# One half of a block's up product: two pieces of one batch each, or two pieces of two batches each between later units

## The chip, the cores and the metric

The kernel runs on 1 core of one Trainium2 chip. The metric is the device time of one execution in microseconds (us), the median of several runs. The core has a matmul engine (TensorE, PE in the profile), a vector engine (VectorE, DVE), a scalar engine (ScalarE, ACT), GpSimd (POOL) and a DMA-issuing engine (SyncE, SP). Each engine works through its own list of instructions in order, and the lists wait for one another by semaphores.

## The reference, cut to what matters

Four batches of 128 rows with 512 features (512 tokens in all) pass through one layer: cross attention to 2048 context rows of each batch, causal self attention with 16 heads over a compressed query, key and value, and a feed-forward part with a shared expert of 1024 inner features and 16 routed experts of 256, of which each token takes four. Each of the three parts adds to the rows.

```python
def relu2(x):
    return jnp.square(jax.nn.relu(x))
...
x = x + _L0_xattn_ref(_layernorm(x, axis=-1), ctx_768, ...)
x = x + _L0_attn_ref(_layernorm(x, axis=-1), ...)
x = x + _L0_ffn_ref(_layernorm(x, axis=-1), ...)
...
shared = relu2(x2 @ shared_up.T) @ shared_down.T
out = routed + shared
```

The change concerns `x2 @ shared_up.T`, for the first 256 of the 1024 inner features and the first 256 of the 512 tokens.

## The kernel before, in words

The shared expert is cut into four blocks of 256 inner features. A block's up product has 256 inner features (two tiles of 128, `m` = 0 and 1) and sums over 512 features (four chunks of 128, `c`). Every float product is made in three matmuls (`split_mm`, line 1604): both operands are kept as a high part and a remainder, and high times low, high times high and low times high are summed in PSUM. So one tile `m` takes 4 x 3 = 12 matmuls whatever the number of tokens, and each has a weight load of its own.

For blocks 0 and 1 the up product is cut by tokens too: the half of batches 0 and 1 (256 tokens), which fits into one PSUM bank for both tiles `m`, is computed while the self attention of the later batches is still running; the other half comes after it. `up_half(e, h, m)` (line 1717) computes tile `m` of half `h` of block `e` in 12 matmuls with 256 columns of tokens. `up_rows(e, m, b)` (line 1728) computes tile `m` for batch `b` alone, in 12 matmuls with 128 columns. Before, block 0's first half is made by `up_rows`, batch 0 first and batch 1 later; block 1's first half by `first_up` (line 1737), which calls `up_half`.

Self attention is cut into 16 units, four for each batch, each of four heads. For a unit, in order:

- TensorE computes its scores, two units at a time (`pair_scores`, line 1750), into one of the banks that `hs_bank` (line 426) names in turn. `pair_scores(14)` waits until `unit_exp(12)` has read the bank before it.
- VectorE masks them and finds the row maxima (`mask_and_max`, line 1116).
- ScalarE takes the exponentials (`unit_exp`, line 847: four pairs of an ACTIVATE and a read of the accumulator, L856).
- VectorE inverts the sums (`inverse_sums`, L1125), and GpSimd multiplies the weights by them (`unit_weights`, L631).
- TensorE transposes the weights into the one bank `B_W` (`unit_T`, line 1765, L1772), after ScalarE has copied out the unit before, and ScalarE copies them out (`unit_copy`, line 841, L845).
- After each batch's four units TensorE multiplies by the values (`unit_sums`, line 1823, L1831), ScalarE and VectorE take the result's two parts (`attended_hi`, L835, and `attended_lo`, L1331), and TensorE projects it (`project`, line 1835).

The order of all this is written out by hand, one list for each engine. TensorE's list around the change is in the program below, from `sums_T(3)` on. ScalarE's list in the same stretch is `unit_exp(12)`, the copy of transposed rows for batch 1 (`rows_hi`, L749), `unit_copy(10)`, `unit_copy(11)`, `unit_exp(13)`, `router_exp(1)`, `attended_hi(2)`, `unit_exp(14)`, `unit_copy(12)`, `unit_exp(15)`, and the copies of units 13 to 15. Then comes `relu_half(0, 0)` (line 772, L777), the first reader of the up product, which waits for semaphore `up_mm`.

GpSimd makes the remainder of block 0's up weights (`half_low`, line 639, L643), and `rows_lo` (line 1095, L1097) the remainder of the normalised rows; both are operands of the product.

Of the kernel before, what the change touches and what calls it, by code (L numbers as in the profile page):

```python
# [25 lines left out]
P = 128  # L26
# [10 lines left out]
def layer_program(nc, x, ctx_in, ctxT_in, wqT, wkT, wv, wd, wu, woT, experts, bq, bk, bv, gate, bias_e,  # L37
                  gammas_betas, out):
    NB, S, D = x.shape
    NKEY, TD = ctx_in.shape[1:]  # L40
    DC = D // P
# [12 lines left out]
    IC = 2  # L54
# [24 lines left out]
    with ExitStack() as es:  # L79
        def sb(name, shape, dt=F32):  # L80
            return es.enter_context(nc.sbuf_tensor(name, shape, dt))
# [7 lines left out]
        def sem(name):  # L89
            return es.enter_context(nc.semaphore(name))  # L90
# [27 lines left out]
        xT_h = sb("xT_h", [P, DC, T], F32R)  # L118
        xT_l = sb("xT_l", [P, DC, T], F32R)
# [91 lines left out]
        def aT(b, i):  # L211

            return (aT_first if b < NB // 2 else aT_last)[:, i, :]
# [12 lines left out]
        def hw_of(u):  # L226

            return hw[:, u % 2, :] if u < 2 * ROWS else hw_more[:, u % 4, :]

        def u_part(e, i):  # L230

            return u_w[e][:, i, :]
# [48 lines left out]
        def small(name, shape, dt=F32):  # L281
# [36 lines left out]
        bank = [es.enter_context(nc.psum_tensor(f"bank{i}", [P, 512], F32)) for i in range(8)]  # L318
# [16 lines left out]
        var_ok, rstd_ok, xn_ok, xT_mm, xhi_ok, xlo_ok = (sem(n) for n in ("var_ok", "rstd_ok", "xn_ok", "xT_mm", "xhi_ok", "xlo_ok"))  # L335
# [7 lines left out]
        qkv_mm, qkv_ok, hs_mm, hnb_ok, exp_ok, hrd_ok, hw_ok, hwT_mm, hwT_ok, a_mm, ahi_ok, alo_ok, wo_mm, x2_ok = (sem(n) for n in (  # L343
            "qkv_mm", "qkv_ok", "hs_mm", "hnb_ok", "exp_ok", "hrd_ok", "hw_ok", "hwT_mm", "hwT_ok", "a_mm", "ahi_ok", "alo_ok", "wo_mm", "x2_ok"))
        lg_mm, rexp_ok, sel_ok, cnt_mm, cnt_ok, ent_ok, ent_mm, idx_ok = (sem(n) for n in (
            "lg_mm", "rexp_ok", "sel_ok", "cnt_mm", "cnt_ok", "ent_ok", "ent_mm", "idx_ok"))
        up_mm, relu_ok, sq_ok, g_ok, acc_mm, base_ok, y_out = (sem(n) for n in (
            "up_mm", "relu_ok", "sq_ok", "g_ok", "acc_mm", "base_ok", "y_out"))
# [10 lines left out]
        ulo_first, dlo_first = sem("ulo_first"), sem("dlo_first")  # L359
# [6 lines left out]
        def tok(b):  # L366
            return slice(b * S, (b + 1) * S)
# [19 lines left out]
        def rows_bank(b):  # L387

            return 1 if b < NB - 1 else B_S

        def wo_bank(b):

            return 1 if b == NB - 2 else B_S
# [4 lines left out]
        HT_TOK = T // 2  # L398
# [4 lines left out]
        def half_bank(e, h):  # L403

            return B_UP[e][0] if h else B_UP[0][e]

        def half(h):
            return slice(h * HT_TOK, (h + 1) * HT_TOK)
# [26 lines left out]
        def unit_at(step, lag):  # L435
# [5 lines left out]
        order = sorted([(POST + 1 + NCH * b, "middle", b) for b in range(NB)] +  # L441
                       [(WO_STEP + 1 + NCH * b, "last", b) for b in range(NB)])
        norm_no = {(kind, b): NB + i for i, (_, kind, b) in enumerate(order)}

        PAIR, COPIED = 2, NQ - 1
# [1155 lines left out]
        def _(pe):  # L1601
            mm = nc.tensor.matmul

            def split_mm(dst, a, b, start, stop):

                mm(dst, a[0], b[1], start=start, stop=False)  # L1606
                mm(dst, a[0], b[0], start=False, stop=False)  # L1607
                return mm(dst, a[1], b[0], start=False, stop=stop)  # L1608

            def rows_T(n, dst):  # L1610
                pe.wait_ge(xn_ok, n + 1)
                for c in range(DC):
                    last = nc.tensor.transpose(dst[:, c * P:(c + 1) * P], xn[:, n % 2, c * P:(c + 1) * P], ident[:])
                last.then_inc(xT_mm, 1)
# [34 lines left out]
            for h in range(DC):  # L1649
                for i in range(2):  # L1650
                    last = mm(bank[B_ROW][0:2, 0:TDB], bq2[:, h, :], wk2[:, i, h, :], start=h == 0 and i == 0, stop=h == DC - 1 and i == 1)
# [11 lines left out]
            for part in range(2):  # L1663
                pe.wait_ge(xlo_ok, 2 * part + 2)
                o = slice(part * HB, (part + 1) * HB)
                for c in range(DC):
                    for t in range(TC):
                        if part == 0:
                            pe.wait_ge(mlo_ok, min(c + 1 + (c == 0 and t == 2), DC))
                        last = split_mm(bank[B_QK[part][t]][:, 0:HB], (M2[:, 0, c, t * P:(t + 1) * P], M2[:, 1, c, t * P:(t + 1) * P]),  # L1670
                                        (xT_h[:, c, o], xT_l[:, c, o]), c == 0, c == DC - 1)
# [5 lines left out]
            for c in range(DC):  # L1677
                mm(bank[B_ROW][0:2, :], M2[:, :, c, TD], xT_h[:, c, :], start=c == 0, stop=False)
                last = mm(bank[B_ROW][0:2, :], M2[:, :, c, TD], xT_l[:, c, :], start=False, stop=c == DC - 1)
# [37 lines left out]
            def up_half(e, h, m):  # L1717

                pe.wait_ge(ulo_first, 2 * e + 2)
                for c in range(DC):  # L1720
                    o = c * IC * P + m * P
                    last = split_mm(bank[half_bank(e, h)][:, m * HT_TOK:(m + 1) * HT_TOK],
                                    (u_part(e, 0)[:, o:o + P], u_part(e, 1)[:, o:o + P]),
                                    (xT_h[:, c, half(h)], xT_l[:, c, half(h)]), c == 0, c == DC - 1)
                if m == IC - 1:
                    last.then_inc(up_mm, 1)

            def up_rows(e, m, b):

                for c in range(DC):  # L1730
                    o = c * IC * P + m * P
                    last = split_mm(bank[half_bank(e, 0)][:, m * HT_TOK + b * S:m * HT_TOK + (b + 1) * S],
                                    (u_part(e, 0)[:, o:o + P], u_part(e, 1)[:, o:o + P]),
                                    (xT_h[:, c, tok(b)], xT_l[:, c, tok(b)]), c == 0, c == DC - 1)
                return last

            def first_up(e, m):
                pe.wait_ge(xlo_ok, norm_no["last", 1] + 1)
                pe.wait_ge(exp_ok, UNITS - 2)
                up_half(e, 0, m)  # L1740
# [9 lines left out]
            def pair_scores(u):  # L1750

                b, r = divmod(u, ROWS)
                pe.wait_ge(qkv_ok, 3 * b + 2)
                if u > 2 * ROWS:
                    pe.wait_ge(exp_ok, u - 1)
                elif u >= 2:
                    pe.wait_ge(exp_ok, u)
                for j in range(HT):
                    for i in range(2):
                        rows = slice((r + i) * DH, (r + i + 1) * DH)  # L1760
                        o = slice(j * P, (j + 1) * P)
                        last = mm(bank[hs_bank(u + i)][:, o], qk_s[rows, 0, o], qk_s[rows, 1, o], start=True, stop=True)  # L1762
                last.then_inc(hs_mm, 2)

            def unit_T(u, step=TAIL):
                pe.wait_ge(hw_ok, u + 1)
                if step - LAG < G:
                    pe.wait_ge(wT_ok, step - LAG + 1)
                else:
                    pe.wait_ge(hwT_ok, u)  # L1770
                for j in range(HT):
                    last = nc.tensor.transpose(bank[B_W][:, j * P:(j + 1) * P], hw_of(u)[:, j * P:(j + 1) * P], ident[:])  # L1772
                last.then_inc(hwT_mm, 1)
# [61 lines left out]
            def project(b):  # L1835
                pe.wait_ge(w_lo, LO_O)
                pe.wait_ge(alo_ok, b + 1)
                if b < 2:
                    pe.wait_ge(qkv_ok, 3 * (b + 2))
                elif b < NB - 1:  # L1840
                    pe.wait_ge(rexp_ok, b)
                else:
                    pe.wait_ge(qkv_ok, 3 * NB)
                for j in range(HT):
                    last = split_mm(bank[wo_bank(b)][:], (aT(b, 0)[:, j * P:(j + 1) * P], aT(b, 1)[:, j * P:(j + 1) * P]),
                                    (wo_w[:, 0, j * D:(j + 1) * D], wo_w[:, 1, j * D:(j + 1) * D]), j == 0, j == HT - 1)
                last.then_inc(wo_mm, 1)
# [45 lines left out]
            for step in range(1, TAIL):  # L1893
# [22 lines left out]
                if 0 <= g < G:  # L1916
                    b, c = divmod(g, NCH)
# [4 lines left out]
                    for k in range(KT):  # L1922
                        last = mm(bank[B_O][:, 0:TD], wT[:, g % 2, k * P:(k + 1) * P], ring[:, g % RING, k, :],  # L1923
                                  start=(c == 0 and k == 0), stop=(c == NCH - 1 and k == KT - 1))
# [29 lines left out]
            unit_T(10)  # L1954
            pe.wait_ge(rexp_ok, 1)
            rows_T(norm_no["last", 1], bank[rows_bank(1)])
            pe.wait_ge(ulo_first, 2)
            pe.wait_ge(xlo_ok, norm_no["last", 0] + 1)
            pe.wait_ge(qkv_ok, 3 * NB - 1)
            for m in range(IC):  # L1960
                up_rows(0, m, 0)
            pair_scores(14)
            unit_T(11)
            router(1)
            unit_sums(2)
            unit_T(12)
            pe.wait_ge(xlo_ok, norm_no["last", 1] + 1)
            for m in range(IC):
                last = up_rows(0, m, 1)
            last.then_inc(up_mm, 1)  # L1970
            unit_T(13)
            project(2)
            unit_T(14)
            first_up(1, 0)
# [164 lines left out]
            for b in range(NB):  # L2139
                for i in range(NL):  # L2140
                    pe.wait_ge(ylo_ok, i + 1)
                    mm(bank[B_END[b]][:], of_token[:, i, tok(b)], ys_h[:, (NG - NL + i) % NYS, :], start=False, stop=False)
                    last = mm(bank[B_END[b]][:], of_token[:, i, tok(b)], ys_l[i][:], start=False, stop=i == NL - 1)
# [53 lines left out]
```

## Time and profile before

| | us |
|---|---|
| median of 3 runs | 352.87 |
| lowest and highest run | 352.58, 354.71 |
| span of the profiled execution, first to last instruction | 350.9 |
| TensorE busy in that span | 332.0 |
| VectorE busy | 239.4 |
| ScalarE busy | 190.5 |

The profile shows one execution. It gives the span and no separate time for that execution; the median of the runs lies 2.0 us over the span. A busy time counts an instruction from its start to its end, and matmuls overlap in the pipeline, so the distance between the starts of neighbouring matmuls tells more of their cost than the duration of one. The chain of work is followed back from the last instruction: at each step to what released it, or to the instruction before it on its engine.

### The profile page before, as it was taken

Reading aid. Unit: us, or ns where it says so; the run is one execution under the profiler, and the core shown is the slowest. Engines: PE = TensorE matmul, PEld = TensorE weight load, DVE = VectorE, ACT = ScalarE, POOL = GpSimd, SP = SyncE. Lnnn points to the kernel's source line nnn. Section 1 sums busy time; section 2 is a strip of 40 time slices with the busy share of each in tenths; the row PEclk is TensorE's granted clock in tenths of the full one; section 3 lists DMA queues with packets and bytes.
Section 4 is the critical chain, followed back from the end, with each engine's and each line's share of the span. In section 5 each row is a group of like instructions: output and inputs, shape, how many; then the busy total and the mean of one; then the engine's idle time right before and its main releaser. Section 6 shows DMA issues by size and latency. Waiting matters only on the chain.

```text
span 350.9 us, 7040 instructions
## 1 busy us (share of the span) xinstructions
PE 332.0 (95%) x2554; PEld 235.1 (67%) x2554; DVE 239.4 (68%) x475; ACT 190.5 (54%) x428; POOL 98.4 (28%) x114
## 2 busy tenths in 40 slices
PE   6999989999999998999799899999999999999995
PEld 4988756677777755867689789788544444444453
DVE  2885789655489637748975469980556777778486
ACT  2356765525576476466777454302246777777510
POOL 3600400000001311226584140004446865522000
PEclk9899999999999999999999999999999999999999
DMA  7985499986422227018032471799834463321483
GB/s 228 401 336 177 180 370 404 412 282 197 156 99 90 92 91 290 40 45 346 2 121 92 150 270 32 297 375 398 326 104 164 166 205 133 119 96 62 157 323 120
DMA packets 17185, 69.70 MB, mean 199 GB/s; under 512 B 2816, under 2 KB 3328, under 8 KB 14592
## 3 DMA queue, kind: packets, MB, share of 16 engines
q1 hardware_dynamic: 12768, 56.93, 43.2%
q0 software_dynamic: 3520, 11.54, 9.3%
q10 hardware_dynamic: 864, 0.79, 0.7%
q8 instruction: 21, 0.34, 0.4%
q14 instruction: 12, 0.10, 0.1%
HBM read 61.91 MB, written 7.34 MB: 197 GB/s over the span
## 4 chain that ended last, share of the span: by engine, by line
PE 71%; DVE 15%; ACT 7%; issue 4%; DMA 2%; DVEq 0%; POOL 0%; ACTq 0%
PE bank L2068 10%; PE bank L2100 10%; PE bank L1923 8%; PE bank L1606 8%; PE bank L1608 8%; PE bank L1607 8%; PE bank L2037 3%; PE bank L1815 2%; DVE res L1583 2%; DMA raw<-in_wkT 2%; PE bank L1867 2%; PE bank L1772 2%; DVE cT L1296 1%; PE bank L1762 1%; PE bank L2079 1%
## 5 line engine op out<-in xcount | busy, mean ns | idle before, releaser
L1923 PE MATMUL bank<-ring,wT 128*128 128x384 f32 x128 | 44.0, 487 | 0.7 <-ACT wT L898 0.7
L2068 PE MATMUL bank<-WX,xsT 128*32 128x256 f32 (+1 forms) x256 | 36.4, 380 | 0.0
L2100 PE MATMUL bank<-WX,hsT 128*32 128x512 f32 (+1 forms) x128 | 36.2, 595 | 0.0
L692 POOL DMA_INDIRECT xs<-x_rows,from_row x20 | 22.1, 1108 | 48.9 <-DVE to_row L1250 25.2
L1296 DVE TENSOR_TENSOR cT<-ring_T,cT 128x512 fp32r<-128x512 f32 x45 | 30.0, 710 | 6.5 <-ACT cT L756 6.5
L1923 PEld LDWEIGHTS bank<-ring,wT 128*128 128x128 f32 x128 | 23.6, 190 | 14.2 <-ACT wT L898 0.9
L1530 DVE COPY copy<-WX 128x1024 f32 x32 | 21.1, 703 | 13.1 <-PE bank L2100 5.9
L2068 PEld LDWEIGHTS bank<-WX,xsT 128*32 128x32 f32 x256 | 17.1, 110 | 18.8 <-issue 8.4
L756 ACT CAST cT<-ring_T 128x512 fp32r<-128x512 f32 x48 | 27.0, 619 | 4.6 <-PE bank L1608 4.5
L2068 PE MATMUL bank<-copy,xsT 128*32 128x256 f32 x384 | 29.3, 380 | 0.0
L2100 PE MATMUL bank<-copy,hsT 128*32 128x512 f32 x192 | 29.1, 595 | 0.0
L602 POOL TENSOR_TENSOR rstd<-var,mhalf 128x1 f32<-128x1 f32 x12 | 7.5, 625 | 73.3 <-DVE var L1082 73.2
L1537 DVE COPY copy<-WX 128x1024 f32 x32 | 21.4, 711 | 5.9 <-PE bank L2068 3.9
L1506 DVE COPY xsT<-bank 128x512 f32<-128x512 f32 x20 | 13.1, 685 | 14.4 <-PE bank L2037 14.4
L699 POOL DMA_INDIRECT y_rows<-ys,to_row x16 | 18.3, 1142 | 12.8 <-ACT ys L1004 10.1
L2100 PEld LDWEIGHTS bank<-WX,hsT 128*32 128x32 f32 x128 | 8.2, 109 | 20.2 <-issue 19.9
L1028 ACT COPY copy<-WX 128x1024 f32 x16 | 16.8, 1048 | 8.3 <-PE bank L2100 7.1
L1606 PE MATMUL bank<-cT,qk_h 128*128 128x512 f32 x48 | 20.0, 417 | 0.2 <-POOL cT L620 0.2
L1608 PE MATMUL bank<-cT,qk_l 128*128 128x512 f32 x48 | 18.8, 393 | 0.0
L1607 PE MATMUL bank<-cT,qk_h 128*128 128x512 f32 x48 | 18.8, 391 | 0.0
L1606 PE MATMUL bank<-xT_l,u_w 128*128 128x256 f32 (+2 forms) x56 | 17.9, 320 | 0.0
L1607 PE MATMUL bank<-xT_h,u_w 128*128 128x256 f32 (+2 forms) x56 | 17.4, 312 | 0.0
(296 smaller groups left out, 883.4 us busy)
## 6 DMA issues: line engine op xcount, KB each, us to landing
WX<-in_experts SPq DMA_DIRECT2D x16, 1024.0 KB, 6.9
ring_T<-in_ctxT SPq DMA_DIRECT2D x16, 768.0 KB, 7.3
ring<-in_ctx SPq DMA_DIRECT2D x16, 768.0 KB, 5.1
WX<-y_rows SPq DMA_DIRECT2D x4, 1024.0 KB, 8.1
raw<-in_experts SPq DMA_DIRECT2D x3, 1024.0 KB, 5.0
raw<-in_wqT SPq DMA_DIRECT2D x4, 256.0 KB, 5.7
res<-in_x SPq DMA_DIRECT2D x4, 256.0 KB, 8.1
raw<-in_woT SPq DMA_DIRECT2D x1, 1024.0 KB, 5.8
```

The lines of the kernel that those rows point to most:

```text
L692: nc.gpsimd.indirect_dma_start(out=xs[:, s % NXS, :], out_offset=None, in_=x_rows, in_offset=bass.IndirectOffsetOnAxis(ap=from_row[:, s:s ...
L699: nc.gpsimd.indirect_dma_start(out=y_rows, out_offset=bass.IndirectOffsetOnAxis(ap=to_row[:, s:s + 1], axis=0), in_=ys[:, s % NYS, :], in_ ...
L756: copy(cT[:, g % 2, 0, t, :], ring_T[:, g % RING_T, t, :]).then_inc(cThi_ok, 1)
L1296: V_.tensor_tensor(cT[:, g % 2, 1, t, :], ring_T[:, g % RING_T, t, :], f32(cT[:, g % 2, 0, t, :]), ALU.subtract).then_inc(cTlo_ok, 1)
L1530: V_.tensor_copy(copies[n % NC][:], WX[:, bass.ds(middle[g][q - 1] * (2 * HALF), HALF)]).then_inc(up_copied, 1)
L1537: V_.tensor_copy(copies[n % NC][:], WX[:, bass.ds(values[q - 1] * (2 * HALF) + HALF, HALF)]).then_inc(down_copied, 1)
L1606: mm(dst, a[0], b[1], start=start, stop=False)
L1607: mm(dst, a[0], b[0], start=False, stop=False)
L1608: return mm(dst, a[1], b[0], start=False, stop=stop)
L1923: last = mm(bank[B_O][:, 0:TD], wT[:, g % 2, k * P:(k + 1) * P], ring[:, g % RING, k, :], start=(c == 0 and k == 0), stop=(c == NCH - 1 an ...
L2068: last = mm(bank[B_H[g % 2]][q * SLOT:(q + 1) * SLOT, 0:IC * P], xsT[:, g % 2, c * P + q * SLOT:c * P + (q + 1) * SLOT], w, start=c == 0, ...
L2100: last = mm(bank[B_Y[g % 2]][q * SLOT:(q + 1) * SLOT, :], hsT[:, g % 2, m * P + q * SLOT:m * P + (q + 1) * SLOT], w, start=m == 0, stop=m ...
```

## The change

The function for one batch goes. Block 0's first half is computed by `up_half` in two pieces, one for each tile `m`, both after unit 12: one between units 12 and 13, the other between units 13 and 14. The piece that stood between the transposes of batch 1's rows and `pair_scores(14)` has nothing in its place.

```diff
-            def up_rows(e, m, b):
-
-                for c in range(DC):
-                    o = c * IC * P + m * P
-                    last = split_mm(bank[half_bank(e, 0)][:, m * HT_TOK + b * S:m * HT_TOK + (b + 1) * S],
-                                    (u_part(e, 0)[:, o:o + P], u_part(e, 1)[:, o:o + P]),
-                                    (xT_h[:, c, tok(b)], xT_l[:, c, tok(b)]), c == 0, c == DC - 1)
-                return last
-
...
             unit_T(10)
             pe.wait_ge(rexp_ok, 1)
             rows_T(norm_no["last", 1], bank[rows_bank(1)])
-            pe.wait_ge(ulo_first, 2)
-            pe.wait_ge(xlo_ok, norm_no["last", 0] + 1)
-            pe.wait_ge(qkv_ok, 3 * NB - 1)
-            for m in range(IC):
-                up_rows(0, m, 0)
             pair_scores(14)
             unit_T(11)
             router(1)
             unit_sums(2)
             unit_T(12)
             pe.wait_ge(xlo_ok, norm_no["last", 1] + 1)
-            for m in range(IC):
-                last = up_rows(0, m, 1)
-            last.then_inc(up_mm, 1)
+            pe.wait_ge(qkv_ok, 3 * NB - 1)
+            up_half(0, 0, 0)
             unit_T(13)
+            up_half(0, 0, 1)
             project(2)
             unit_T(14)
             first_up(1, 0)
```

## Rows read from the trace of the kernel before

**Rows 1.** The page: span, and busy time of each engine.

```profile
span 350.9 us, 7040 instructions
...
PE 332.0 (95%) x2554; PEld 235.1 (67%) x2554; DVE 239.4 (68%) x475; ACT 190.5 (54%) x428; POOL 98.4 (28%) x114
```

**Rows 2.** The page: the chain that ended last, by engine.

```profile
PE 71%; DVE 15%; ACT 7%; issue 4%; DMA 2%; DVEq 0%; POOL 0%; ACTq 0%
```

**Rows 3.** The chain in order of time around the change: start us, us, what.

```profile
176.49 0.04 issue
176.53 1.16 PE bank L1762 x16
...
180.11 0.06 PE bank L1606
...
182.74 1.09 PE bank L1762 x16
183.83 0.58 PE bank L1772 x4
...
185.66 1.01 PE bank L1831 x32
186.66 0.59 PE bank L1772 x4
187.25 0.06 PE bank L1606
...
189.88 0.46 PE bank L1772 x4
190.34 0.23 PE bank L1606
...
193.52 0.12 PE bank L1606
...
194.93 0.44 PE bank L1772 x4
```

**Rows 4.** PE by line and shape, 179 to 206 us: mean ns of one.

```profile
L1606 PE MATMUL bank<-xT_l,u_w 128*128 128x128 f32 x16 | 4.5, 279 | 0.0
...
L1606 PE MATMUL bank<-xT_l,u_w 128*128 128x256 f32 x8 | 2.4, 302 | 0.0
```

**Rows 5.** ACT in order of time, 181 to 196 us.

```profile
181.83 0.21 ACT L856 ACTIVATION_READ_ACCUMULATOR hw_more<-bank,hnb 128x1 f32 x1
...
182.39 0.62 ACT L845 COPY hwT_last<-bank 128x512 f32<-128x512 f32 x1
...
186.73 0.59 ACT L835 CAST aT_last<-bank 128x512 fp32r<-128x512 f32 x1 [0.21 <-PE bank L1831]
...
188.60 0.61 ACT L845 COPY hwT_last<-bank 128x512 f32<-128x512 f32 x1
...
195.89 0.61 ACT L777 ACTIVATE act<-bank 128x512 f32<-128x512 f32 x1
```

**Rows 6.** DVE in order of time: remainder of batch 1's rows, mask of unit 14.

```profile
182.68 0.66 DVE L1097 TENSOR_TENSOR xT_l<-bank,xT_h 128x512 fp32r<-128x512 f32 x1
183.88 0.69 DVE L1105 SCALAR_TENSOR_TENSOR masked<-bank,upper 128x512 uint8<-128x512 f32 x1 [0.54 <-PE bank L1762]
```

**Rows 7.** POOL in order of time: the weights of unit 13.

```profile
186.74 1.04 POOL L631 TENSOR_TENSOR hw_more<-hw_more,hrd 128x512 f32<-128x512 f32 x1 [1.57 <-DVE hrd L1125]
```

**Rows 8.** PE in order of time, first 10 us: its longest wait between matmuls.

```profile
7.82 0.95 PE L1630 MATMUL bank<-wk,UW 128*128 128x386 f32 x4 [1.74 <-ACT UW L787]
```

**Rows 9.** Stretches: engines' busy times, then granted clock (1.00 is full), DMA share, GB/s.

```profile
9.00:10.00 1.00, 0.84 (x3) 0.84 (x4) 0.70 (x2) 0.63 (x2) 0.58 (x1) 0.64 1.09 390
10.00:12.00 2.00, 2.00 (x8) 2.00 (x7) 1.56 (x5) 1.78 (x4) 1.52 (x2) 0.50 1.09 418
12.00:13.00 1.00, 1.00 (x6) 1.00 (x5) 0.97 (x5) 0.00 (x0) 0.85 (x1) 0.65 0.99 410
198.00:200.00 2.00, 1.11 (x7) 0.81 (x6) 0.69 (x1) 1.98 (x4) 0.00 (x0) 1.00 1.01 379
```

## The prediction

> **What bounds the kernel now.** I read the page's busy times first: TensorE is busy for 332.0 of 350.9 us, the next engine for 239.4 [rows 1]. The reader is to see that only TensorE can be the bound of the whole, and then to distrust the 95%: a matmul's busy time overlaps its neighbours', so the engine can be busy by the page and still wait inside that time, and a cheaper instruction is not worth its busy time. Second comes the chain that ended last: 71% of it is TensorE, 15% VectorE, 7% ScalarE [rows 2]. Third, the chain in order of time around the edit: from 180.11 us to 194.93 us each piece is TensorE's, with no hole, and both pieces that the change takes out lie on it [rows 3]. So before, TensorE's own list sets the time there, and what is saved on it counts until another engine's result is awaited. The question is therefore which result comes last once the list is shorter, and the three lists of ScalarE, VectorE and GpSimd answer it [rows 5 to 7].
>
> **What goes and what comes, on TensorE alone.** Removed are two pieces of 24 matmuls with 128 columns. The first runs from 180.11 to 182.74, the second from 187.25 to 189.88, 2.63 us each, which is 0.110 us for a matmul [rows 3]. Added are two pieces of 12 matmuls with 256 columns. The same function already runs for block 1: 12 matmuls from 193.52 to 194.93, 1.41 us, 0.117 us for each [rows 3]. So twice the columns cost 7 ns more, and TensorE is spared 2 x 2.63 - 2 x 1.41 = 2.44 us. The durations of one, 279 and 302 ns, would have given 48 x 0.279 - 24 x 0.302 = 6.1 us; they overlap and are not the price [rows 4].
>
> A rule of the Trainium skill speaks against the saving. Its page TensorE: Matmul & The Clock Gate, section Back-to-back issue gap, gives the isolated distance of two matmuls as the columns over 2.4 GHz and 2.5 ns more, thus about 56 ns at 128 columns and 109 ns at 256; by it 48 x 0.056 = 2.7 us would go and 24 x 0.109 = 2.6 us would come, an estimate by that page, and the change would only move work. The trace does not agree at 128 columns: it shows 110 ns there, twice that figure.
>
> **First wait, between 180.11 and `pair_scores(14)`.** The piece for batch 0 stood in a place where TensorE would otherwise have waited. `pair_scores(14)` overwrites the bank that `unit_exp(12)` reads, and the last accumulator read of that unit ends at 181.83 + 0.21 = 182.04 [rows 5]. From the end of a ScalarE result to TensorE's next work the chain shows 0.04 us, and the 16 score matmuls then take 1.16 us [rows 3]. So after the change they run from 182.08 to 183.24, where before they ended at 183.83: of the 2.63 us removed here, 0.59 are gained and 1.97 become a wait from 180.11 to 182.08. What ends there is not itself moved: `unit_exp(12)` hangs on `mask_and_max(12)`, ahead of everything that waits for `pair_scores(14)` in VectorE's list.
>
> **The stretch after it moves 0.59 us forward.** `unit_T(11)` 0.58 (to 183.82), the router of batch 1 184.41 to 185.66, thus 1.25 (to 185.07), `unit_sums(2)` 1.00 (to 186.07), `unit_T(12)` 0.59 (to 186.66) [rows 3]. None of these meets another wait: `unit_T(11)` needs the copy that ends at 182.39 + 0.62 = 183.01 [rows 5], the router the remainder that ends at 182.68 + 0.66 = 183.34 [rows 6]. VectorE's mask of unit 14 started 0.05 us after the scores, at 183.88 [rows 6], so it follows them forward to 183.29. Then the first new piece takes 1.41 (to 188.07). Its waits are long met: the high rows, weights and bank that it needs were ready for the piece before.
>
> **Second wait, between the first new piece and `unit_T(13)`.** There is one bank for the transposes, and `unit_T(13)` needs `unit_copy(12)` to have emptied it. That copy is not late because of `unit_T(12)`. It stands in ScalarE's list behind `attended_hi(2)` and `unit_exp(14)`, and before it ran from 188.60 to 189.21 [rows 5]. `attended_hi(2)` starts at 186.73, 0.06 us after `unit_sums(2)` ended [rows 3, 5], so this run of ScalarE moves forward by the same 0.59: the copy runs from 188.01 to 188.62, and TensorE goes on at 188.66. Before, the 2.63 us piece covered this copy with 0.67 us to spare (it ended at 189.88). The new one is 1.22 us shorter, and 0.59 us of waiting appears (188.07 to 188.66). GpSimd's weights of unit 13 are no rival here: they ended at 186.74 + 1.04 = 187.78 before and follow forward [rows 7].
>
> Behind the waiting `unit_T(13)` in TensorE's list stand the second new piece, `project(2)` and `unit_T(14)`. They need nothing later than that copy. So: 188.66 + 0.46 (`unit_T(13)`) + 1.41 (second piece) = 190.53. Before, `project(2)` began at 190.34 [rows 3]. The sum: 2.44 us of work saved, 1.97 + 0.59 us of new waits, and 0.07 us more for scores that start from a standstill (1.16 against 1.09) [rows 3]; together 0.19 us later.
>
> **What hangs on the moved pieces besides.** The up product is now complete at 190.53, not 189.88. Its reader on ScalarE starts at 195.89, behind the copies of units 13 to 15 [rows 5], so 5.4 us of cover remain. The step issues no DMA and passes no queue of SP or GpSimd. From 190.53 on the order is as before, and the chain runs through TensorE, so I carry 0.19 us to the end undiminished: 350.9 + 0.2 = 351.1 for the span. The profiled span lies 2.0 us under the median of the runs, which I take as unchanged: 353.1 us.
>
> **Bounds of what no row shows.** The two waits don't exist before. The first is certain to some hundredths, since its releaser does not move. The second hangs on five ScalarE instructions keeping their distances. If the copy came early enough the wait would vanish and `project(2)` start 0.59 us sooner, 0.4 us earlier than before; if ScalarE fell behind by as much, 0.8 us later. With these ends the median would be 352.5 to 353.7. I take the middle, since all distances on ScalarE come from rows.
>
> **Rivals.**
>
> *The saving comes through whole.* If neither wait lasted, 2.44 us would be gained: 350.4 us. For it: the stretch is all TensorE on the chain. Against it: `unit_exp(12)` ends at 182.04 whatever TensorE does [rows 5].
>
> *The clock falls in the first wait (the slower side).* The longest wait between matmuls before is 1.74 us, up to 7.82 us [rows 8]; from then on the granted clock went from full to 0.50 and came back. The stretches 9 to 13 us show 0.64, 0.50, 0.50 and 0.65, which at two levels (1.00, that is 2.4 GHz, and 0.50, 1.2 GHz) is 0.72 + 2.00 + 0.70 = 3.4 us at the lower one, with half of it lost, 1.7 us [rows 9]. The new wait, 1.97 us, is longer than that one. If it has the same effect, the work behind it takes 1.7 us longer, ScalarE's list follows, and the time is 353.1 + 1.7 = 354.8 us. Against it: the early wait came in the first 8 us of the kernel, while here the chain shows the engine at work without a hole up to the wait, and after it [rows 3]. At 198 to 200 us it worked for only 1.11 of 2 us, and the clock stayed at 1.00 [rows 9]. It decides from the point at which the clock falls at all; a shorter first wait would not show it.
>
> The Trainium skill's page on TensorE, section HAM oscillation — how this bites in real kernels, describes kernels in which waits between bursts of matmuls send the clock down each time. The trace agrees with it at 9 us and shows no such fall later.
>
> *The wide pieces cost by their columns*, so that 256 cost twice 110 ns: each new piece would take 2.64 us, the second wait would vanish, and `project(2)` would start at 186.66 + 2.64 + 0.46 + 2.64 = 192.40, 2.1 us late: 355.0 us. The rows of block 1's pieces at 117 ns are nearly proof against it [rows 3].
>
> **How the numbers follow.** I give 0.80 to the forecast, whose own range is 352.4 to 353.8; 0.08 to the whole saving; 0.10 to the fallen clock; 0.02 to the wide pieces' price. The runs before spread from 352.58 to 354.71, skewed upward. The range that should hold 8 in 10 goes from 352.0, half way to the whole saving, to 354.8, the fallen clock. A measurement of this kernel tells about 1%, or 3.5 us, from no change. No case reaches it on the faster side: all of the work saved is 2.44 us, so 0.02. On the slower side a fallen clock that lasts twice as long would come near, so 0.03. That leaves 0.95 for no change.
>
> **What would show each step right or wrong.** Right: 24 matmuls of 256 columns about 0.117 us apart for block 0; a TensorE wait of about 2 us before the scores of units 14 and 15, released by ScalarE's exponentials (L856); a second of about 0.6 us before `unit_T(13)`, released by the copy at L845; `project(2)` within 0.5 us of 190.5; the granted clock at 1.00 throughout. Wrong: the first wait under 1.5 us, the second missing, a granted clock below 1.00 between 182 and 188 us, or a shift that is there at 190 us and gone at the end.

## The result and the profile after

The changed kernel takes 355.63 us (median of 22 runs, 353.15 to 357.21); the kernel before, run beside it, takes 353.09 us (22 runs, 351.75 to 354.71). The ratio is 1.006, with a 95% interval of 1.0043 to 1.0076: slower by 0.6%. The profiled execution took 356.8 us, with a span of 355.0 us. In every ratio here the runs more than 1.5% over the fastest of their kernel are left out; for three of the experiments (e3_gap_only, e4_early, f1_split) that takes out the long runs which they are about, so there the median of all runs is what counts.

The page of the changed kernel, span and busy times, to be held against [rows 1]:

```profile
span 355.0 us, 6992 instructions
...
PE 335.5 (95%) x2530; PEld 237.6 (67%) x2530; DVE 239.8 (68%) x475; ACT 190.6 (54%) x428; POOL 97.8 (28%) x114
```

TensorE has 24 matmuls less and is busy for 3.5 us more. Something has made its instructions longer. The chain in order of time shows where (L1753 are the scores, L1763 the transposes of a unit, L1822 the sums of a batch):

```profile
180.78 1.25 ACT hw_more L856 x7
182.03 0.14 issue
182.17 2.08 PE bank L1753 x16
184.24 1.04 PE bank L1763 x4
185.29 0.01 PE bank L1606
...
187.65 1.87 PE bank L1822 x32
189.52 1.05 PE bank L1763 x4
190.56 0.21 PE bank L1606
...
192.66 0.44 PE bank L1763 x4
193.10 0.12 PE bank L1606
...
194.51 0.23 PE bank L1606
```

Against [rows 3] the reader is to see the same list of work at nearly twice the price: the scores take 2.08 us and not 1.16, unit 11 takes 1.04 and not 0.58, the sums 1.87 and not 1.01. From 192.66 us on all has its old price: unit 13 takes 0.44, and the second wide piece behind it goes from 193.10 to 194.51, 1.41 us. `project(2)` begins at 194.51, where before it began at 190.34, 4.17 us later; the two spans differ by 4.1 us.

The waits of TensorE, the longest first:

```profile
PE bank L1753 <- ACT hw_more L856: 2.4, 1, 2.4
PE bank L1618 <- DVE wT L1265: 1.5, 1, 1.5
```

The new wait is now the longest of all. The stretches around it in the changed kernel (engines' busy times, then the granted clock, DMA share, GB/s):

```profile
164.00:169.00 5.00, 4.58 (x52) 3.58 (x49) 4.55 (x8) 3.15 (x11) 2.64 (x3) 0.66 0.06 25
169.00:180.00 11.00, 9.66 (x69) 7.47 (x67) 8.43 (x22) 7.82 (x25) 5.83 (x7) 1.00 0.02 8
180.00:182.00 2.00, 0.00 (x0) 0.00 (x0) 1.93 (x5) 1.48 (x9) 1.95 (x3) 0.93 0.45 131
182.00:184.00 2.00, 1.83 (x16) 1.81 (x16) 1.32 (x3) 0.99 (x3) 2.00 (x3) 0.50 0.87 324
184.00:186.00 2.00, 2.00 (x12) 1.83 (x10) 1.65 (x3) 0.67 (x2) 1.14 (x1) 0.50 0.41 172
186.00:188.00 2.00, 2.00 (x16) 1.95 (x20) 1.14 (x3) 1.50 (x9) 0.39 (x1) 0.50 0.71 236
188.00:190.00 2.00, 2.00 (x35) 1.54 (x24) 1.55 (x3) 0.42 (x1) 0.65 (x1) 0.50 0.07 27
190.00:192.00 2.00, 2.00 (x11) 2.00 (x10) 0.87 (x2) 2.00 (x11) 0.13 (x1) 0.51 0.00 0
```

And in the profile of the kernel before:

```profile
180.00:190.00 10.00, 10.00 (x120) 9.59 (x120) 8.29 (x16) 7.81 (x35) 6.67 (x7) 1.00 0.55 180
```

After the change TensorE does nothing from 180 to 182 us, the clock goes to the lower level (0.50, 1.2 GHz) inside that stretch, at 181.7 us, and stays there until 192 us: 0.28 + 8.00 + 1.96 = 10.2 us. TensorE is busy in all of the eight microseconds from 184 on, and they count as no hole in the chain. There is another low stretch, 3.4 us between 164 and 169 us, ahead of the change; what it costs is read below.

### The profile page after: what moved, and what is told of

Its sections match the earlier page's. It is cut to its first block, busy times and chain, and to the rows that moved or that the text cites. A ratio compares the mean times of both kernels' runs of the same rounds, so it can differ in the third digit from the quotient of the medians.

```text
span 355.0 us, 6992 instructions
## 1 busy us (share of the span) xinstructions
PE 335.5 (95%) x2530; PEld 237.6 (67%) x2530; DVE 239.8 (68%) x475; ACT 190.6 (54%) x428; POOL 97.8 (28%) x114
## 4 chain that ended last, share of the span: by engine, by line
PE 70%; DVE 16%; ACT 7%; issue 3%; DMA 2%; POOL 1%; DVEq 0%; ACTq 0%
PE bank L2054 10%; PE bank L2086 10%; PE bank L1914 8%; PE bank L1606 8%; PE bank L1608 7%; PE bank L1607 7%; PE bank L2023 3%; DVE res L1583 2%; DMA raw<-in_wkT 2%; PE bank L1806 2%; PE bank L1858 2%; PE bank L1763 1%; DVE cT L1296 1%; PE bank L1822 1%; PE bank L1753 1%
## 5 line engine op out<-in xcount | busy, mean ns | idle before, releaser
L1028 ACT COPY copy<-WX 128x1024 f32 x16 | 16.8, 1047 | 8.3 <-PE bank L2086 7.1
L1033 ACT COPY copy<-WX 128x1024 f32 x16 | 16.7, 1042 | 0.0
L1606 PE MATMUL bank<-xT_l,u_w 128*128 128x256 f32 (+1 forms) x48 | 16.4, 341 | 0.0
```

## The experiments

Two theories stand against each other. **A:** the wait ahead of the scores lets TensorE's clock fall, and the light steps behind it (16 score matmuls of 32 rows, four transposes, 12 router matmuls of 16 columns, the sums) leave it low. **B:** the new order costs the time by its two waits on ScalarE, and the clock is a bystander. Each kernel is compared with the kernel before on the same chip. The median of the kernel before alone goes from 353.09 to 354.24 us between the rows, so times are compared inside a row, and rows by their ratios.

| run | edit | us, median of all (range) | kernel before | ratio and interval |
|---|---|---|---|---|
| changed kernel | | 355.63 (353.15 to 357.21) | 353.09 | 1.006 (1.0043 to 1.0076) |
| e1_fill17 | wait filled, 17 matmuls | 354.34 (353.71 to 355.03) | 353.39 | 1.0029 (1.0014 to 1.0045) |
| e1_fill8 | wait filled, 8 matmuls | 355.22 (353.24 to 357.72) | 354.24 | 1.0035 (1.0007 to 1.0063) |
| e2_mixed | one tile in the early place | 354.07 (353.30 to 358.57) | 353.39 | 1.0033 (1.0004 to 1.0062) |
| e3_gap_only | kernel before, early piece left out | 358.83 (353.25 to 360.75) | 353.39 | 1.003 (0.999 to 1.0069) |
| e4_early | wide pieces one place earlier | 353.83 (352.40 to 360.31) | 353.39 | 1.001 (0.9981 to 1.0039) |
| f1_split | wide pieces between light steps | 354.22 (351.37 to 357.61) | 353.81 | 0.9972 (0.9947 to 0.9997) |
| f2_split_fill | f1_split and filled | 353.49 (351.81 to 354.62) | 353.81 | 0.9997 (0.9974 to 1.002) |

**The wait filled** (against the changed kernel).

```diff
             rows_T(norm_no["last", 1], bank[rows_bank(1)])
+            pe.wait_ge(ulo_first, 2)
+            pe.wait_ge(xlo_ok, norm_no["last", 0] + 1)
+            pe.wait_ge(qkv_ok, 3 * NB - 1)
+            for _ in range(17):
+                mm(bank[half_bank(0, 0)][:, 0:P], u_part(0, 0)[:, 0:P], xT_h[:, 0, tok(0)], start=True, stop=True)
             pair_scores(14)
```

> The changed kernel with 17 matmuls of 128 columns whose result is overwritten, put where the piece for batch 0 stood (1.9 us of work in a wait of 2.0 us; nothing of the product is left out). Theory A, the clock: with TensorE at work there, the granted clock stays at 1.00 from 180 to 195 us; project(2) starts near 190.5 us as forecast, and the time is 0.998 to 1.002 of the kernel before. Theory B, the order: the two waits on ScalarE cost the time by themselves and the clock is a bystander; the ratio stays at 1.006.

The order and its dependences on ScalarE are those of the changed kernel, TensorE has 17 matmuls more to do, and the time is less, by the ratios (1.0029 against 1.006) some 1.1 us. B's 1.006 lies outside the interval: that speaks against B. But A's number was missed too, 1.0029 where at most 1.002 was expected, and so was its full clock. The stretches of the profiled run say why:

```profile
180.00:182.00 2.00, 1.73 (x16) 1.59 (x15) 1.97 (x4) 1.39 (x9) 1.96 (x3) 1.00 0.39 135
182.00:184.00 2.00, 1.74 (x23) 1.65 (x23) 1.92 (x5) 1.08 (x4) 2.00 (x3) 1.00 0.87 311
184.00:186.00 2.00, 2.00 (x33) 1.98 (x35) 1.60 (x3) 1.95 (x10) 1.24 (x2) 0.86 0.47 197
186.00:188.00 2.00, 2.00 (x26) 1.62 (x18) 1.86 (x4) 1.15 (x6) 1.04 (x1) 0.50 0.75 240
188.00:190.00 2.00, 2.00 (x15) 2.00 (x15) 1.12 (x3) 2.00 (x12) 0.76 (x1) 0.79 0.06 23
```

The clock now holds through the wait's place, of which 0.53 us is left, and falls later, at 185.4 us, for 3.4 us: through the sums and the transposes of unit 12 and into the first wide piece. TensorE had been at work without a hole since the scores began at 182.26 us. So a fall without the long wait is seen here; the kernel before shows one without any wait further down.

Half the filler, 8 matmuls in place of 17:

> The changed kernel with 8 matmuls of 128 columns in the first wait in place of 17 (0.9 of 2.0 us filled, a wait of about 1.1 us stays; nothing of the product is left out). Theory A, the clock goes with the length of the wait: the median lies between the filled kernel and the changed one, ratio 1.003 to 1.006, and runs above 356 us are rare. Theory B: 1.006 as in the changed kernel.

By its ratio, 1.0035, this kernel can't be told from the filled or from the changed one. In its profile a wait of 1.23 us is left, and the clock is low for 6.8 us (0.98, 0.50, 0.50, 0.50, 0.82 over the five stretches of 2 us from 182 to 192 us), between the 3.4 and the 10.2 us of the other two. One of its 11 runs was above 356 us; 7 of the changed kernel's 22 were.

**The wait alone** (against the kernel before). This kernel does not compute block 0's up product for batch 0.

```diff
-            for m in range(IC):
-                up_rows(0, m, 0)
             pair_scores(14)
```

> The kernel before with batch 0's piece left out and nothing in its place (the up product of block 0 for batch 0 is not computed): the first wait alone, without any piece of 256 columns and without the second wait. Theory A, the clock: the wait of 2 us brings the clock down as in the changed kernel, and the ratio is 1.003 to 1.006 although TensorE does 2.6 us less work. Theory B, the order: 24 matmuls are saved, the scores start 0.6 us earlier, there is no second wait, and the ratio is 0.997 to 0.999.

Block 0 has no piece of 256 columns here and there is no second wait, TensorE has 24 matmuls less than before, and the median of all its runs is 5.4 us higher (358.83 against 353.39), the largest difference of all the runs. Eight of the twelve took over 358 us; none of the 35 runs of the kernel before beside them took over 354.82. TensorE's wait and the clock of the profiled run, 360.75 us:

```profile
182.62 0.80 PE L1762 MATMUL bank<-qk_s 32*128 32x128 f32 x4 [2.38 <-ACT hw_more L856]
```

```profile
182.00:192.00 10.00, 9.38 (x75) 8.69 (x75) 6.76 (x12) 5.58 (x26) 4.63 (x5) 0.52 0.45 157
192.00:200.00 8.00, 8.00 (x32) 7.33 (x32) 0.35 (x2) 2.50 (x11) 2.08 (x2) 0.53 0.01 2
```

The low stretch lasts some 17 us here (9.6 of the ten microseconds, then 7.5 of eight), two thirds longer than in the changed kernel, and it outlasts the piece for batch 1 behind unit 12, whose 24 matmuls of 128 columns run from 191.01 to 196.03 us, nearly twice their price; it ends at 199.5 us among the 512-column matmuls of `project(2)`. B wanted 0.997 to 0.999. The ratio of 1.003 does not quite exclude that, as its interval begins at 0.999; the medians and the profile go against B. The size was not foreseen by A either.

**One tile in the early place** (against the kernel before). Tile 0 for batch 0 stays where it was, tile 1 becomes one wide piece.

```diff
-            for m in range(IC):
-                up_rows(0, m, 0)
+            up_rows(0, 0, 0)
             pair_scores(14)
...
-            for m in range(IC):
-                last = up_rows(0, m, 1)
-            last.then_inc(up_mm, 1)
+            up_rows(0, 0, 1)
+            up_half(0, 0, 1)
             unit_T(13)
```

> Tile 0 as in the kernel before (batch 0 in the early place, batch 1 after unit 12), tile 1 as one piece of 256 columns after unit 12, both ahead of unit 13. Theory A, the clock: 12 matmuls fill 1.3 of the 2.0 us, a wait of about 0.7 us stays, the clock holds, the scores of units 14 and 15 start 0.6 us earlier than before, TensorE's list is 1.2 us shorter, and project(2) starts at about 189.9 instead of 190.3: ratio 0.998 to 0.999, and lower than the changed kernel by 0.7%. Theory B, the order: the scores start as in the changed kernel, so the ratio is 1.004 to 1.006.

The scores did start early, at 181.92 us after a wait of 1.0 us, yet the ratio is 1.0033: a miss for A as I had put it, and no verdict against B, whose 1.004 to 1.006 lies inside the interval. In its profile the clock held through the wait and then was low for 3.4 us from 184.8 us, as in the filled kernel: the long fall is missing there, the short one is not. Three of the twelve runs, of 355.69 to 358.57 us, were longer, and none of them has a profile.

**Wide pieces among the light steps** (against the changed kernel). The first variant moves each piece up by one place, the second also puts the router behind unit 12, and the third adds the 17 fillers to the second.

```diff
             unit_T(11)
-            router(1)
-            unit_sums(2)
-            unit_T(12)
             pe.wait_ge(xlo_ok, norm_no["last", 1] + 1)
             pe.wait_ge(qkv_ok, 3 * NB - 1)
             up_half(0, 0, 0)
-            unit_T(13)
+            unit_sums(2)
+            unit_T(12)
+            router(1)
             up_half(0, 0, 1)
+            unit_T(13)
             project(2)
```

The diff is that of f1_split, in which ScalarE's `router_exp(1)` goes behind `unit_copy(12)`; in e4_early the router stays ahead of the sums and ScalarE's list as it was.

> The changed kernel with the two pieces of 256 columns moved up by one place each: the first right behind unit 11, ahead of the router and the sums of batch 2, the second behind unit 12. The first wait is as in the changed kernel. Theory A1, the clock falls in the wait and comes back when wide matmuls run: the first piece now runs 3 us earlier, and the lower clock lasts 3 to 7 us instead of 10 us; ratio 1.001 to 1.004. Theory A2, the clock stays down for some 10 us whatever is run: ratio 1.006 as in the changed kernel. Theory B, the order alone: by the rows project(2) starts at 190.5 us in either kernel, so the ratio is that of the changed kernel, 1.006.

> The changed kernel with its two wide pieces put between the light steps: scores, unit 11, first piece, sums of batch 2, unit 12, router, second piece, unit 13; the router's exponentials move behind unit 12's copy on ScalarE. The first wait stays. Theory A, the clock: wide matmuls stand 2 us behind the wait, so the low clock is rarer and shorter than in the changed kernel: median 353 to 354.5 us, ratio 0.999 to 1.003. With the clock at 1.00 project(2) starts near 189.9 us, as the second wait is covered. Theory B, the order: 0.6 us faster than the changed kernel by the second wait alone, ratio 1.004.

> The same, and the first wait filled with 17 matmuls of 128 columns whose result is overwritten. Theory A, the clock: neither the wait nor a long run of light steps is left from 160 us on behind unit 10; the granted clock stays at 1.00 from 180 to 195 us and project(2) starts at 189.9 to 190.1 us: ratio 0.997 to 0.999, the fastest of all so far. Theory B, the order: the filler changes nothing against the version without it.

Without the filler the first two spread wide: seven of e4_early's twelve runs lie between 352.4 and 353.9 us and five between 356.1 and 360.3; f1_split has five runs below 352.5 us and five from 355.9 us up. With the filler nothing is above 354.62 us. So the wide pieces are no safe cure while the wait stands; where the clock holds, the order itself is no slower than before. The median of all of e4_early's runs is 0.1% above that of the kernel before, as A1 had it and against the 1.006 of A2 and B; the 3 to 7 us at the lower clock that A1 wanted are not in its profile. The profile of f1_split, a run of 355.94 us, has a low stretch of 3.4 us from 184.6 us on:

```profile
184.00:186.00 2.00, 2.00 (x14) 2.00 (x13) 1.89 (x4) 1.31 (x6) 1.88 (x2) 0.65 0.82 344
186.00:188.00 2.00, 2.00 (x26) 1.71 (x28) 1.56 (x4) 0.68 (x4) 1.03 (x1) 0.50 0.45 137
```

The first wide piece runs inside it, from 184.65 to 187.15 us, 2.50 us and not 1.41: its 12 matmuls of 256 columns did not keep the clock up there. The profile of f2_split_fill shows the order at full clock and `project(2)` at 190.06 us, as expected (189.9 to 190.1):

```profile
180.00:195.00 15.00, 14.78 (x147) 13.64 (x146) 10.11 (x21) 9.47 (x40) 8.41 (x9) 1.00 0.33 118
234.00:238.00 4.00, 4.00 (x12) 3.12 (x11) 1.18 (x9) 0.00 (x0) 1.83 (x2) 0.57 1.01 424
```

The same profile has a low stretch of 3.4 us at 234 us, far behind the change, and its span is 352.5 us, not below 350.9. Its ratio of 0.9997 can't be told from 1. The ratio of f1_split is 0.9972, but the median of all its runs is 0.4 us above that of the kernel before. No version here beats both kernels with certainty.

The profile of e4_early has the full clock from 169 us past the change too, although the first wait is there with 2.17 us, and it has the second wait, on the copy of unit 12:

```profile
190.37 0.63 PE L1763 MATMUL bank<-ident,hw_more 128*128 128x128 f32 x4 [0.66 <-ACT hwT_last L845]
```

**The changed kernel again**, three more profiles of it unchanged.

> The changed kernel once more, unchanged, for a second profile. Theory A, the clock: the wait of some 2 us ahead of the scores is there again; where the granted clock falls behind it, project(2) starts 2 us or more after 190.5 us, and where it stays at 1.00, project(2) starts at 190.3 to 190.7 us with a wait of 0.6 us ahead of unit 13, as the rows gave. Theory B, the order: project(2) starts later than 192 us with the clock at 1.00.

> The changed kernel, unchanged, for a third profile. Theory A: project(2) starts 0 to 0.5 us behind 190.5 us if the clock holds from 180 to 192 us, and otherwise later by half the time at the lower clock, less up to 0.6 us that the second wait gives back. Theory B: project(2) starts after 192 us whatever the clock.

> The changed kernel, unchanged, for a fourth profile; the same as the third.

Their times were 354.29, 356.69 and 353.71 us, their spans 352.5, 355.0 and 352.0 us. The second has a low stretch of 10.2 us from the wait on, like the first profile; the other two have 3.4 us from 185 us on, and `project(2)` starts at 191.83 us in the first of them, 1.3 us behind 190.5 where A had put 2 or more. No profile of four shows the clock at full from 180 to 192 us throughout. The last of them, in the chain and by stretches:

```profile
182.43 1.16 PE bank L1753 x16
...
185.41 1.86 PE bank L1822 x32
187.28 1.05 PE bank L1763 x4
...
189.96 0.63 PE bank L1763 x4
...
191.88 0.12 PE bank L1608
```

```profile
184.00:186.00 2.00, 2.00 (x29) 1.92 (x30) 1.76 (x3) 1.79 (x9) 1.40 (x2) 0.82 0.65 270
186.00:188.00 2.00, 2.00 (x29) 1.55 (x21) 1.69 (x4) 0.94 (x5) 1.04 (x1) 0.50 0.70 190
188.00:190.00 2.00, 2.00 (x15) 1.83 (x14) 1.28 (x3) 2.00 (x11) 0.37 (x1) 0.82 0.18 72
```

The scores are at full pace here, 1.16 us, although TensorE had waited 2.28 us ahead of them; the sums are not. `project(2)` starts at 192.00 us.

**The kernel before again**, five more profiles of it, since its own runs fall into two groups.

> The kernel before once more, unchanged, for a second profile. Its runs fall into two groups, 352 to 353.4 us and 354 to 354.8 us. Theory A, the clock: the group is made by stretches of lower granted clock that differ from run to run; a run of the upper group shows one stretch of 3.4 us more at half clock between 160 and 195 us than the profile at hand, a run of the lower group none. Theory B: the groups come from something else, and the granted clock is 1.00 from 13 us on in either.

> The kernel before, unchanged, for a third profile. If this run is of the upper group (354 us and more), theory A wants a stretch of lower clock of 3.4 us between 160 and 240 us that the first two profiles (352.9 and 353.0 us) did not have; if of the lower group, none. Theory B: no difference in the clock.

> The kernel before, unchanged, once more, for a profile of a run of its upper group. Theory A: such a run has its 3.4 us at the lower clock among the light steps behind the scores of units 14 and 15 (184 to 189 us), where the filled kernel has it too, and project(2) starts 1.5 to 1.8 us later than the 190.3 us of the other profiles. Theory C, the groups of the kernel before come from elsewhere: the clock stays at 1.00 there, and the 1.5 us appear in another stretch. A run of the lower group shows neither.

> The kernel before, unchanged, once more; theories A and C as for the fourth profile: 3.4 us at the lower clock between 184 and 189 us if this run is of the upper group, or a full clock there.

> The kernel before, unchanged, once more; theories A and C as for the fourth profile: 3.4 us at the lower clock between 184 and 189 us if this run is of the upper group, or a full clock there.

The first four took 353.0, 352.98, 352.66 and 352.48 us, with spans from 350.7 to 351.2 us and a full clock from 169 us to the last two microseconds. The last took 354.58 us with a span of 352.8 us, a run of the upper group. Its stretches:

```profile
164.00:169.00 5.00, 4.57 (x56) 3.55 (x53) 4.79 (x8) 3.21 (x12) 3.05 (x3) 0.66 0.17 72
184.00:186.00 2.00, 2.00 (x28) 1.98 (x31) 1.93 (x3) 1.46 (x7) 1.57 (x2) 0.98 0.63 262
186.00:188.00 2.00, 2.00 (x31) 1.62 (x24) 1.57 (x4) 1.12 (x7) 1.04 (x1) 0.50 0.56 203
188.00:190.00 2.00, 2.00 (x15) 2.00 (x13) 1.58 (x4) 2.00 (x11) 0.22 (x1) 0.67 0.18 68
```

It has the same 3.4 us (0.08 + 2.00 + 1.32) from the sums on, without any wait ahead of the scores, and its `project(2)` starts at 192.04 us, 1.70 us later than in [rows 3]. The third, at 352.66 us, has the low stretch between 164 and 169 us as well, and a full clock behind it:

```profile
164.00:169.00 5.00, 4.57 (x54) 3.57 (x53) 4.54 (x8) 2.95 (x12) 2.92 (x3) 0.66 0.15 62
186.00:188.00 2.00, 2.00 (x37) 1.80 (x30) 1.57 (x4) 1.79 (x10) 1.04 (x1) 1.00 0.67 223
```

Its span is 350.9 us, that of the first profile to a tenth, but the early stretch is not free: this run came to it 0.44 us sooner and left with that lead gone. The distance from VectorE's step ahead of it (L1336) to the scores of units 12 and 13 behind it shows the cost, the kernel before first (its scores start at 176.53 [rows 3]), then the changed kernel:

```profile
161.39 0.70 DVE res L1336
160.66 0.70 DVE res L1336
176.23 1.16 PE L1753 MATMUL bank<-qk_s 32*128 32x128 f32 x16 [0.25 <-ACT qk_s L873]
```

That is 15.14 us without the stretch and 15.57 with it. In all the seven profiles without it the distance is 15.10 to 15.14 us, in the ten with it 15.54 to 15.57: it costs 0.4 us. All four profiles of the changed kernel have it, and two of six of the kernel before. The change stands behind it in the order, and no run shows whether it has to do with the change.

Each run also has its mean granted clock on record, without a profile. Of the 74 runs of the kernel before that the experiments brought, the 36 with a mean of 0.992 or more took at most 353.52 us, and of the 38 with 0.990 or less all but one took at least 353.81 us. So the two groups go with the clock; a mean does not say where in the run it was low.

So in one of six profiles the kernel before has a low stretch of 3.4 us between 184 and 190 us; the changed kernel has one in four of four, and in two of them it begins at the wait and lasts 10.2 us.

## Why the prediction was wrong, step by step

**The price of the matmuls was right.** The second wide piece takes 1.41 us for 12 matmuls in the changed kernel, 0.117 us each at the full clock. The isolated distance in the Trainium skill's page TensorE: Matmul & The Clock Gate, section Back-to-back issue gap, is not borne out at 128 columns, where [rows 3] have 110 ns; at 256 the estimate of 109 ns by its formula is near the 117 ns of these rows.

**The first wait was right in place and releaser, and a little longer.** 1.97 us were forecast and 2.36 measured: in that execution TensorE came to it 0.3 us sooner, and it took 0.14 us, not 0.04, from ScalarE's last accumulator read to the scores.

**The second wait is real, but the changed kernel's profiles hardly show it.** It needs a TensorE at full clock. In e4_early, where the clock held, 0.66 us of it appear. In the changed kernel the low clock made TensorE as late as the copy or later: where the low stretch lasted 10.2 us, unit 13 took its 0.44 us; where it lasted 3.4 us, 0.61 and 0.63 in place of 0.46, a rest of that wait.

**The sum for a full clock is borne out as far as a run shows it.** No profile of the changed kernel had a full clock there. f2_split_fill, with the order changed and the wait filled, had one, and began `project(2)` where its expectation, worked out from the same rows, had put it. The fastest run of the changed kernel, 353.15 us, whose mean granted clock was 0.995 as in the profile of before, is near the 353.1 us forecast; it has no profile, and the mean does not say where its clock was low.

**What failed is the choice between the cases: the step "The clock falls in the first wait", to which I gave 0.10.** It was the case that came, in two of four profiles in the wait itself, in the other two behind it. Two arguments against it were bad. One was that at 198 to 200 us TensorE worked for only 1.11 of 2 us with the clock at 1.00 [rows 9]: one stretch in one execution, and the fall differs from run to run of the same code. The other was that the engine is "at work without a hole" behind the wait [rows 3]. It is, but with scores, transposes, 16-column router matmuls and sums, and through those the clock stayed low in these profiles, or fell with no wait at all, as the kernel before itself showed in its slowest profiled run. I had only the profile of a run without that fall, and the upper run of the three at 354.71 us was before me as a number that I took for noise.

**In the same step the price was too small.** I took 3.4 us at the lower clock from [rows 9] and 1.7 us for it. For a stretch of 3.4 us that is nearly right. From the scores to unit 13 the kernel before takes 7.14 us in [rows 3] and 8.75 in its profile with the stretch, 1.61 more; the changed kernel's last profile takes 7.53 (182.43 to 189.96) where the prices of [rows 3] give 5.99, 1.54 more. But in two of four profiles the stretch was 10.2 us, and `project(2)` began 194.51 - 190.53 = 3.98 us late in the first of them. There the same steps took 10.49 us (182.17 to 192.66) and not 5.99, 4.50 more. With 0.09 for the later scores, less the 0.59 of the second wait, which vanished, and 0.02 for unit 13, that is the 3.98 us. It is less than half of the 10.2 us because some of the stretch lies inside the wait and the steps wholly at the lower clock took 1.8 to 1.9 times as long, not twice. The 354.8 us of this case had left the second wait in. The early low stretch of [rows 9] was a poor model of the length: it is a single one of 3.4 us, and here the lengths differ from run to run.

The median of 355.63 us lies 0.8 us above the range's upper end, 354.8, which was set by the 1.7 us. Eight of the 22 runs lie between 355.1 and 356.0 us, the median among them, with a mean clock of 0.985 to 0.987, and none of the four profiles is of such a run. The nearest is the profile of e1_fill8, at 355.22 us and 0.986, with its 6.8 us at the lower clock; that the median stands for a stretch of that length is likely from this, and not shown. The range's lower end was worked out wrongly too, half way from 353.1 to 350.4 us being 351.75 and not 352.0, but nothing came of that.

The Trainium skill's page TensorE: Matmul & The Clock Gate, section HAM oscillation — how this bites in real kernels, tells of a clock that goes down in waits between bursts of matmuls. Two of the changed kernel's four profiles agree, the first with a fall at 181.7 us in a wait of 2.36 us; in the other two the clock held through waits of 2.29 and 2.28 us. The fall with TensorE busy is shown by the runs here alone.

**"Within 1%" was right**, and so was that the shift at `project(2)` comes through to the end: 4.17 us there, 4.1 us in the span.

What stays open: why one run of the same code falls at a given place and the next does not, and how the 3.4 us among the light steps could be had to stay away for good. A rival to the wait, the moment at which the steps run, was not tested: no run kept the wait and moved only its time. That they come in half of the runs of the kernel before is read from one profile of its upper group and from the times and mean clocks of its two groups.

## What to carry to other kernels

Work that fills a wait of TensorE can be worth more than its own result: taking 24 matmuls out of a place where TensorE then mostly waits brought the scores 0.57 us forward in the first profile, and in two of four profiles the clock fell there for 10 us. Before removing such work, read the granted clock over the steps that follow, in several profiles: here it stayed low through scores, transposes, router matmuls of 16 columns and sums, and in single runs through 12 matmuls of 256 columns or 24 of 128, while the profile counted TensorE as busy. And where the runs of a kernel fall into two groups, take a profile of each before calling the difference noise.

## What was not expected of the hardware

The granted clock fell with TensorE busy in 2.00 of every 2 us, in the kernel before (0.50 from 186 to 188 us) and in the filled kernel. The low stretches measured 3.4, 6.8, 10.2 and some 17 us. And a low stretch of 3.4 us at 164 us, in ten of seventeen profiles, cost 0.4 us each time, although TensorE waits for other engines there, and a comparison of whole runs (352.66 us with it, 352.48 without) does not show it.
